# Four graph layers on one core: clearing the sums on GpSimd between stages, and splitting the last relu-and-add over ScalarE and GpSimd

## What is computed

```python
x = _layernorm(x + _L0_gnn_ref(x, ...))   # relu(sum over edges of (x @ W[relation])[src] * weight)
x = _layernorm(x + _L1_gnn_ref(x, ...))   # relu(x @ W + sum over edges of (x @ M)[src])
x = _layernorm(x + _L2_gnn_ref(x, ...))   # attention over the edges, 4 heads, weights by node and edge type
x = _layernorm(x + _L3_gnn_ref(x, ...))   # two normalised graph convolutions with a residual product
...
def _L3_gnn_ref(x, edge_index, W, b, resW, resb):
    ...
    for l in range(W.shape[0]):
        h = x @ W[l]
        agg = segment_sum(norm[:, None] * h[src], dst) + b[l]
        x = relu(agg + x @ resW + resb)      # x_res is the layer's input
    return x
```

## Time and profile before

| | us |
|---|---|
| median of 3 runs | 4201.42 (4199.71 to 4203.07) |
| the profiled execution, its own time | 4203.95 |
| its span in the trace | 4202.1 |
| `first_layer_nodes`, about 1081.0 to 1121.5 | 40.5 |
| first part of `attention_tables`, 1620.8 until the first product by type at about 1680 | 59.2 |
| `last_nodes`, 4159.4 to the end | 42.7 |

### The profile page before, as it was taken

One profiled execution on the slowest core, in us unless ns is written; L12 is line 12 of the kernel. 1 busy time (PEld: TensorE's weight loads), 2 busy tenths in 40 slices (PEclk: granted clock), 3 DMA queues, 4 the chain that ended last, 5 costly groups with the idle time before them and its releaser, 6 DMA issues. The chain is left out here.

```text
span 4202.1 us, 64286 instructions
## 1 busy us (share of the span) xinstructions
PE 3172.8 (76%) x11666; PEld 2176.1 (52%) x11666; DVE 2231.3 (53%) x7567; ACT 894.9 (21%) x2584; POOL 2744.3 (65%) x2879
## 2 busy tenths in 40 slices
PE   5999938877788873886888878888886777676764
PEld 2444426666566642333676767777544444444442
DVE  8200047666666645344888857766663443433435
ACT  1333300000200000441444555555320000100000
POOL 3777767777677774334777747777317777477774
PEclk9999969889899986997878768777898877888776
DMA  4333323333333334566555535555313333333332
GB/s 141 141 148 146 145 71 105 106 106 105 95 106 106 106 107 145 224 246 231 165 164 165 165 94 161 163 162 163 82 46 105 105 105 105 99 105 106 106 105 90
DMA packets 226896, 540.00 MB, mean 129 GB/s; under 512 B 73482, under 2 KB 107948, under 8 KB 212876
## 3 DMA queue, kind: packets, MB, share of 16 engines
q0 software_dynamic: 136528, 374.97, 30.3%
q1 hardware_dynamic: 57880, 103.46, 6.8%
q10 hardware_dynamic: 32164, 57.91, 4.6%
HBM read 390.04 MB, written 146.09 MB: 128 GB/s over the span
## 5 line engine op out<-in xcount | busy, mean ns | idle before, releaser
L579 POOL DMA_INDIRECT gcn_edges_g<-table,rows_i x782 | 741.1, 948 | 429.4 <-ACTq L844 191.8
L892 PE MATMUL ps<-gcn_edges_g,gcn_edges_onehot 128*128 x1760 | 627.6, 496 | 308.5 <-SPq L590 274.5
L937 DVE TENSOR_TENSOR acc<-acc,ps 128x256 f32 (+1 forms) x880 | 369.4, 420 | 751.9 <-PE ps L892 740.4
L892 PEld LDWEIGHTS ps<-gcn_edges_g,gcn_edges_onehot 128*128 128x128 f32 x1760 | 391.0, 242 | 537.6 <-issue 484.3
L305 POOL DMA_INDIRECT records<-rec,slots x391 | 376.2, 962 | 184.7 <-issue 124.0
L579 POOL DMA_INDIRECT sum_g<-table8v,rows_i x391 | 379.7, 971 | 163.0 <-issue 112.2
L579 POOL DMA_INDIRECT rel_g<-table,rows_i x391 | 372.1, 952 | 135.0 <-issue 96.9
L579 POOL DMA_INDIRECT score_g<-table8k,rows_i x391 | 371.3, 950 | 135.1 <-issue 112.7
L579 POOL DMA_INDIRECT conv_edges_g<-table,rows_i x391 | 371.6, 950 | 127.4 <-issue 93.8
L357 PE MATMUL ps<-w,xt 128*128 128x512 f32 x1000 | 435.8, 595 | 18.3 <-ACT xt L327 18.3
L1016 PE MATMUL ps<-q,onehot_t 128*128 x880 | 320.5, 500 | 113.2 <-DVE onehot_t L1114 111.9
(11 more groups left out here) (315 smaller groups left out, 4778.5 us busy)
## 6 DMA issues: line engine op xcount, KB each, us to landing
table<-tb SPq DMA_DIRECT2D x50, 1280.0 KB, 4.5
score_dst_bc<-dst_rows ACTq DMA_DIRECT2D x110, 256.0 KB, 3.5
sum_dst_bc<-dst_rows ACTq DMA_DIRECT2D x110, 256.0 KB, 3.5
gcn_edges_g<-table,rows_i POOLq DMA_INDIRECT x782
table<-gcn_tb SPq DMA_DIRECT2D x50, 128.0 KB, 1.7
records<-rec,slots POOLq DMA_INDIRECT x391
rel_g<-table,rows_i POOLq DMA_INDIRECT x391
conv_edges_g<-table,rows_i POOLq DMA_INDIRECT x391
```

What stands on the lines that cost most here:

```text
L579: pool.indirect_dma_start(out=m.g[:, 2 * (p % RING) + j, 0:D], out_offset=None, in_=table, in_offset=bass.IndirectOffsetOnAxis(ap=m.rows_i ...
L892: mm = pe.matmul(bank(m, i % BANKS, 0, width), m.onehot[:, 2 * k + j, :], window(m.g, slot + j, 0, width), start=(j == 0), stop=(j == 1))
L937: nc.vector.tensor_tensor(acc, acc, bank(m, i % BANKS, 0, width), ALU.add).then_inc(added, 1)
```

## The change

It has three parts. In `first_layer_nodes` the clearing of `m.acc` moves from VectorE to GpSimd: tile by tile, once `norm.normed` says that the tile is normed, and ahead of the indirect DMA of the same tile. In `attention_tables` the same, ahead of the indirect DMA of `x`. In `last_nodes` relu goes to ScalarE (it writes `h[:, t, :]`, semaphore `cut`) and the addition of `x` to GpSimd (it reads `h` and `m.x`, writes `m.acc`); VectorE starts the norm of a tile two iterations later in relation to L1612, and the square root on ScalarE stands four tiles behind its relu.

```diff
 # first_layer_nodes
         @block.gpsimd
         def _(pool):
             for t in range(NT):
+                pool.wait_ge(norm.normed, t + 1)
+                nc.gpsimd.memset(m.acc[:, t, :], 0.0)
                 pool.indirect_dma_start(
...
-            for i in range(NT + 6):
-                t = i - 6
-                if 0 <= t < NT:
-                    dve.wait_ge(norm.normed, t + 1)
-                    nc.vector.memset(m.acc[:, t, :], 0.0)
+            for i in range(NT + 5):
                 norm.vector(dve, i, m.x)
...
 # last_nodes
         @block.scalar
         def _(act):
             for t in range(NT):
+                act.wait_ge(joined, t + 1)
+                nc.scalar.activation(h[:, t, :], m.acc[:, t, 0:D], ACT.Relu).then_inc(cut, 1)
+                norm.root(act, t - 4)
+            for t in range(NT - 4, NT):
                 norm.root(act, t)
+
+        @block.gpsimd
+        def _(pool):
+            for t in range(NT):
+                pool.wait_ge(cut, t + 1)
+                nc.gpsimd.tensor_tensor(m.acc[:, t, 0:D], h[:, t, :], m.x[:, t, :], ALU.add).then_inc(norm.summed, 1)
 
         @block.vector
         def _(dve):
-            for i in range(NT + 7):
-                norm.vector(dve, i - 1, h)
-                if 1 <= i <= NT:
-                    dve.wait_ge(joined, i)
-                    nc.vector.scalar_tensor_tensor(m.acc[:, i - 1, 0:D], m.acc[:, i - 1, 0:D], 0.0, m.x[:, i - 1, :], ALU.max,
-                                                   ALU.add).then_inc(norm.summed, 1)
+            for i in range(NT + 9):
+                norm.vector(dve, i - 3, h)
                 if i < NT:
...
 # attention_tables
             for t in range(NT):
                 pool.wait_ge(norm.normed, t + 1)
+                nc.gpsimd.memset(m.acc[:, t, :], 0.0)
                 pool.indirect_dma_start(
...
                 norm.vector(dve, i - 1, m.x)
-                t = i - 8
-                if 0 <= t < NT:
-                    dve.wait_ge(norm.normed, t + 1)
-                    nc.vector.memset(m.acc[:, t, :], 0.0)
...
-            for t in range(NT - 1, WINDOWS):
+            for t in range(NT, WINDOWS):
                 nc.vector.memset(m.acc[:, t, :], 0.0)
```

More of the change, by code:

```diff
@@ L1585, in last_nodes @@
         norm = TileNorm(ctx, nc, m, "gcn")
-        joined, stored = sems(ctx, nc, "end", "joined", "stored")
-        m.spent += [joined, stored]
+        joined, cut, stored = sems(ctx, nc, "end", "joined", "cut", "stored")
+        m.spent += [joined, cut, stored]
         block = ctx.enter_context(nc.Block())
```

## The result

The changed kernel takes 4227.44 us (median of 6 runs, 4223.79 to 4228.09), the kernel before 4200.69 in the same comparison: ratio 1.0062, 95% interval 1.0049 to 1.0075. The prediction was 4203 with a range to 4217, so the time lies outside it, on the slow side. The profiled execution took 4228.09 us.

A forecast was written before the change was run, and what follows sets the result against it. No engine was full; VectorE set the end of last_nodes and the pace of attention_tables, SP's marks read ended first_layer_nodes. Terms 8.7 + 0.5 - 7.7 = +1.5 us on the median 4201.42 gave 4203 us, range 4190 to 4217.

The forecast's parts named there:

- The sum: Whole kernel: the three changed stages add 8.7 + 0.5 - 7.7 = +1.5 us, giving 4203 us.
- The memset, 0.32: GpSimd memset of 260 columns costs 0.32 us per tile, none hidden in the 0.30 issue; bounds 0 and 0.62.
- Part 1, +8.7: first_layer_nodes: GpSimd's memset-scatter pairs of 1.58 us end last and delay SP's read of the marks by 8.7 us.
- rival 3's first mechanism: Clearing stages: VectorE's norm holds up the memset, making it dearer; at 0.45 total +8.0 us; chance 0.10 without blocking.
- Part 2, +0.5: attention_tables: GpSimd at 1.58 us a pair becomes slower than VectorE at 1.45; last scatter 0.5 us later.
- Part 3, -7.7: last_nodes: the pass leaving VectorE saves 0.32 us a tile, 8.0 in all, less 0.3 for late first statistics.
- the case it took: last_nodes: GpSimd's additions do not block VectorE, tile 1.19 us; with memset 0.32, chance 0.43.
- Rival 1: last_nodes: GpSimd's addition and VectorE's L1616 block each other, tile 1.64 us, +3.3 there, total 4214 us; chance 0.35.
- both bounds: GpSimd addition in last_nodes: from below a one-stream memset, 0.32 us; from above a scatter, 0.96; middle 0.64 taken.
- the list of signs: What to check in the three changed stages: scatters 1.58 apart, SP's read near 1126, last_nodes norms 1.19 or about 1.6 apart.

The follow-up runs named there:

- e9: Kernel before with only the GpSimd clearing in first_layer_nodes and attention_tables, last_nodes as before: 4207.23 us beside 4202.14, ratio 1.0016.
- e4: Kernel before with the changed last_nodes, each GpSimd addition replaced by a 740-column GpSimd memset into a scratch tile: ratio 0.9981, in a batch of longer times.

## Why the prediction was wrong

**The sum.** The step that failed is the one that it never wrote down: "8.7 + 0.5 - 7.7 = +1.5" has a term for each stage that the change touches and none for the others, whose time was taken as fixed. The others gave +19.1 us, through indirect DMAs that all took 7 to 8 ns longer once the program held GpSimd additions. No row ahead of the run could size it, and no rival or bound held it; the ends of the range were made of the three parts alone. With the three measured parts (+5.1) and the rest unchanged the time would have been 4206.5, within the range, though by errors in the parts that offset each other.

**The memset, 0.32 for 0.21.** Its duration was right (0.33 against a line that gave 0.32 from the earlier trace rows). Wrong was the choice that the issue gap can't hide any of it: 0.13 of the 0.30 vanishes when a memset stands between two scatters. (About 0.01 of the 0.21 belongs to the longer scatters: in e9, where they have their old level, a pair is 1.46.) The row used for it, the scatter 0.27 us behind a norm in the earlier trace rows, shows the delay after a wait and not what is left behind an instruction of GpSimd itself.

**Part 1, +8.7, measured +7.7** (e9: +8.0). With pairs of 1.47 the same working gives 1085.06 + 0.27 + 0.33 + 24 x 1.47 = 1120.94, landed at 1123.34, so +6.0. The long memsets (up to 0.49 us) and scatters (up to 1.22) add 2.1: from the first scatter to the last it is 37.35 us (1090.41 to 1127.76) and not 24 x 1.47 = 35.28. The memsets are rival 3's first mechanism, which did appear beside the cheaper memset; the rival had no long scatters. The read behind the last scatter and the stage start behind the read came 0.25 and 0.12 sooner than counted. So the sum was near the measured value by luck: a memset too dear and collisions that were left out nearly met. The structure, that the read of the marks waits for GpSimd and the next stage for the read, was right.

**Part 2, +0.5, measured -1.5** (e9: -1.8). The structure was right, GpSimd becomes the slower one, but at 1.47 a pair and not 1.58. 24 x 0.11 = 2.6 us is taken off, and three longer scatters (1.14 to 1.25 us) give about 0.6 back, which makes the -1.5.

**Part 3, -7.7, measured -1.1.** The arithmetic of the forecast was nearly right for the case it took: without the additions' reads e4 has a tile of 1.17 us against the 1.19 forecast, and its `last_nodes` is 7.05 us shorter than that of before. Part of the 0.65 that is missing lies in the count, since the forecast took 0.32 off all 25 tiles, and the loop in which a join and a norm alternate is only part of the stage.

The case was wrong. Rival 1 had the mechanism and its place, and was kept out of the sum. It had the size too large: it let the whole join (0.47) follow the addition (tile 1.64), and the profile shows a join that ends 0.29 us after the addition. With the measured pieces the chain is 0.29 + 0.03 + 0.42 + 0.07 + 0.72 = 1.53, the measured tile. The addition (0.72) was near the 0.64 taken from both bounds, and relu took 0.42 as in the earlier trace rows.

The stage as a whole, before and after: from the first join to the first norm 5.75 and 5.53 us, from there to the last join 28.23 and 25.41, from there to the last norm 3.83 and 5.70, and to the end 4.84 and 4.87. The middle is shorter because VectorE now runs 8 joins ahead of the first norm instead of 6, which leaves fewer tiles for the loop, and the tail is longer for the same reason. The changes are -0.2, -2.8, +1.9 and 0.0, in sum -1.1.

**What held.** That SP's read of the marks waits for GpSimd and the next stage for that read, and that GpSimd becomes the slower engine in `attention_tables`, came as described, and the places to look were the right ones; what the list of signs lacked was one for the stages that nobody touched.

## What to carry to other kernels

Before giving GpSimd its first tensor operation in a kernel that lives on its indirect DMAs, run the kernel with a few idle one-column operations of that kind and compare the median duration of the gathers; here 7 ns times 2700 outweighed everything that was saved. When comparing two profiles, read first the stages that were not changed, then the others. In this kernel the work taken from a VectorE loop of instructions with two SBUF operands was better placed on ScalarE than on GpSimd, which had to read SBUF for it (join 0.48 beside ScalarE, 0.82 beside the addition).

## What the hardware showed beyond that

- The duration of a GpSimd gather falls on one level for a whole program, with a median of 946, 949, 953 or 957 ns in twenty profiled runs, nearly the same for all its tables and, of the three kernels that ran in two batches, in both.
- A GpSimd memset of 260 columns between two indirect DMAs starts without a gap and shortens the gap of the next from 0.30 to 0.17 us. It takes 0.33 us, and up to 0.51 (e9) where it starts under a running norm of VectorE.
- A GpSimd memset of 0.72 us beside a VectorE instruction with two SBUF operands leaves it at 0.48 us; an addition of the same length makes it 0.82, and it then ends 0.29 us after the addition.
